# Four products of a residual LoRA kernel, from one float32 pass to three fp32r passes of split parts

## The reference

```
x = x + ((x @ B0[id0].T) @ A0[id0].T)                       # layer 0, rank 16
x = x + (x @ W.T + b) + 2 * ((x @ A1[id1]) @ B1[id1])       # layer 1, W is 2048 x 2048
```

## Time and profile before

| | |
|---|---|
| median of 3 runs | 1398.6 us (1396.78 to 1398.95) |
| profiled execution, its own time | 1398.88 us |
| its span, first to last instruction | 1396.9 us |
| PE busy | 1372.8 us, 98% |
| DVE busy | 943.6 us, 68% |
| ACT busy | 529.1 us, 38% |
| float32 products L540 | 8 records for 4 products |

### The profile page before, as it was taken

One profiled execution on the slowest core, in us unless ns is written; L12 is line 12 of the kernel. 1 busy time (PEld: TensorE's weight loads), 2 busy tenths in 40 slices (PEclk: granted clock), 3 DMA queues, 4 the chain that ended last, 5 costly groups with the idle time before them and its releaser, 6 DMA issues.

```text
span 1396.9 us, 16200 instructions
## 1 busy us (share of the span) xinstructions
PE 1372.8 (98%) x6024; PEld 1128.8 (81%) x6024; DVE 943.6 (68%) x1049; ACT 529.1 (38%) x588; POOL 79.1 (6%) x163
## 2 busy tenths in 40 slices
PE   6899999999999999999999999999999999999999
PEld 5788877888888878888888888888888888888887
DVE  4677897777877887687765566665755566665662
ACT  3444444433334443343324453333233444333321
POOL 2012010001010000001001000000101000000000
PEclk9999999999999999999999999999999999999999
DMA  9789764778888987599895335455856343555642
GB/s 343 242 293 306 264 238 147 243 236 282 297 292 307 314 297 264 178 301 327 287 358 194 110 112 180 163 175 168 276 204 189 117 135 134 169 167 189 194 151 83
DMA packets 98591, 311.60 MB, mean 223 GB/s; under 512 B 13009, under 2 KB 14289, under 8 KB 98513
## 3 DMA queue, kind: packets, MB, share of 16 engines
q1 hardware_dynamic: 92736, 298.96, 63.1%
q0 software_dynamic: 5776, 11.61, 2.9%
HBM read 254.94 MB, written 55.57 MB: 222 GB/s over the span
## 4 chain that ended last, share of the span: by engine, by line
PE 91%; DVE 4%; DMA 2%; issue 1%; ACT 1%; SPq 1%; ACTq 0%; DVEq 0%
PE acc L590 27%; PE acc L591 27%; PE acc L592 27%; DMA w_two<-w 2%; PE acc L565 2%; PE down_ps L549 2%; PE down_ps L550 2%; PE image_ps L535 1%; PE image_ps L529 1%; PE image_ps L530 1%; DVE w_one L759 1%; DVE bg_lo L794 1%; DVE w_lo L767 1%; DVE x_lo L789 0%; ACT w_hi L627 0%
## 5 line engine op out<-in xcount | busy, mean ns | idle before, releaser
L590 PE MATMUL acc<-x_hi,w_hi 128*128 128x512 f32 x1792 | 702.1, 392 | 16.3 <-DVE x_lo L789 12.5
L591 PE MATMUL acc<-x_lo,w_hi 128*128 128x512 f32 x1792 | 699.5, 390 | 0.0
L592 PE MATMUL acc<-x_hi,w_lo 128*128 128x512 f32 x1792 | 699.1, 390 | 0.0
L627 ACT ACTIVATE w_hi<-w_one 128x1024 fp32r<-128x1024 f32 x223 | 235.9, 1058 | 541.1 <-PE acc L592 504.5
L767 DVE TENSOR_TENSOR w_lo<-w_one,w_hi 128x1024 fp32r<-128x1024 f32 x223 | 273.1, 1225 | 215.2 <-ACT w_hi L627 215.2
L590 PEld LDWEIGHTS acc<-x_hi,w_hi 128*128 128x128 f32 x1792 | 337.6, 188 | 89.0 <-issue 16.6
L591 PEld LDWEIGHTS acc<-x_lo,w_hi 128*128 128x128 f32 x1792 | 337.6, 188 | 71.7 <-issue 1.0
L592 PEld LDWEIGHTS acc<-x_hi,w_lo 128*128 128x128 f32 x1792 | 337.3, 188 | 71.2
L660 ACT ACTIVATE sums<-acc 128x512 f32<-128x512 f32 x96 | 57.1, 594 | 203.7 <-PE acc L592 188.1
L826 DVE SCALAR_TENSOR_TENSOR sums<-acc,bias_sb,sums 128x512 f32<-128x512 f32 x128 | 95.7, 747 | 22.0 <-PE acc L565 20.8
L759 DVE TENSOR_TENSOR w_one<-w_one,w_two 128x1024 f32<-128x1024 f32 x79 | 96.4, 1220 | 17.1 <-DMA w_two<-w 17.1
(11 more groups left out here) (61 smaller groups left out, 610.3 us busy)
## 6 DMA issues: line engine op xcount, KB each, us to landing
w_one<-w SPq DMA_DIRECT2D x143, 512.0 KB, 5.5
w_one<-w_sums SPq DMA_DIRECT2D x80, 512.0 KB, 3.7
w_two<-w SPq DMA_DIRECT2D x79, 512.0 KB, 7.4
x_stage<-x SPq DMA_DIRECT2D x64, 512.0 KB, 4.4
out<-sums SPq DMA_DIRECT2D x128, 256.0 KB, 4.6
w_sums<-w_one SPq DMA_DIRECT2D x40, 512.0 KB, 4.1
resident<-x SPq DMA_DIRECT2D x32, 512.0 KB, 8.6
bg_raw<-w_rows SPq DMA_DIRECT2D x32, 512.0 KB, 5.0
```

The lines of the kernel that those rows point to most:

```text
L590: pe.matmul(ps[:, :], w_hi[ws][:, c, :], hi, start=(c == 0), stop=False)
L591: pe.matmul(ps[:, :], w_hi[ws][:, c, :], lo, start=False, stop=False)
L592: mm = pe.matmul(ps[:, :], w_lo[ws][:, c, :], hi, start=False, stop=(c == H - 1))
L627: act.activation(w_hi[s % W_PARTS][:, :, :], w_one[s % W_ONES][:, :, :], ACT.Copy).then_inc(w_hi_ready, 1)
```

## The change

The product of the coupling block with the rows becomes three fp32r matmuls, high x high, low x high and high x low. `across` is split once, both parts on DVE, in its loop body at s = 5, in two more instructions that each wait for the one before. The rows are split for each j at the end of the background splits of the bodies s = 5, 8, 11, 14: ACT makes `rows_hi`, DVE `rows_lo`. The PE no longer waits for the rows' DMAs but for `rows_ready`, which DVE gives behind `rows_lo`; ACT waits for the DMAs, and for j > 0 for the PE's product of j - 1. POOL's load of the next rows waits for `rows_ready` in place of the product.

The raw rows, `across` and the third raw background buffer move into parts of `sums` that aren't yet in use at that time; the memory so freed holds the split parts, with padding so that what follows keeps its place. Because of the third raw buffer, DVE's addition of step 14 now waits until chunk 29 is split.

```diff
+ROWS_SPLIT_AT = (5, 8, 11, 14)
...
-            b1_rows = sb("b1_rows", [P, T], F32, early)
+            across_hi, across_lo = (sb(f"across_{k}", [P, P], F32R, early) for k in ("hi", "lo"))
+            sb("before_image", [P, 2 * P], F32, early)
             image = sb("image", [P, T], F32, early)
-            bg_raw.append(sb("bg_raw2", [P, 2, T], F32, early))
+            rows_hi, rows_lo = (sb(f"rows_{k}", [P, T], F32R, early) for k in ("hi", "lo"))
...
-        across = sums[1][:, H - 1, T - P:T]
+        across = sums[1][:, 1, 0:P]
+        b1_rows = sums[1][:, H - 1, :]
+        bg_raw.append(sums[0][:, H - 2:H, :])
...
             def load_rows(j):
                 if j:
-                    pool.wait_ge(b1_rows_used, j)
+                    pool.wait_ge(rows_ready, j)
...
                     if k == (4 if j else 6):
                         pe.wait_ge(across_ready, 1)
-                        pe.wait_ge(b1_rows_loaded, NB * DMA * (j + 1))
-                        pe.matmul(ps[:, :], across, b1_rows[:, :], start=False, stop=False).then_inc(b1_rows_used, 1)
+                        pe.wait_ge(rows_ready, j + 1)
+                        hi, lo = across_hi[:, :], across_lo[:, :]
+                        pe.matmul(ps[:, :], hi, rows_hi[:, :], start=False, stop=False)
+                        pe.matmul(ps[:, :], lo, rows_hi[:, :], start=False, stop=False)
+                        pe.matmul(ps[:, :], hi, rows_lo[:, :], start=False, stop=False).then_inc(b1_rows_used, 1)
...
                 if s:
                     for z in background(s + 1):
                         split_bg(z)
+                if s in ROWS_SPLIT_AT:
+                    j = ROWS_SPLIT_AT.index(s)
+                    act.wait_ge(b1_rows_loaded, NB * DMA * (j + 1))
+                    if j:
+                        act.wait_ge(b1_rows_used, j)
+                    act.activation(rows_hi[:, :], b1_rows, ACT.Copy).then_inc(rows_hi_ready, 1)
...
                     dve.wait_ge(copied, copied_before(s - H) + 1)
                     if g:
                         dve.wait_ge(out_stored[o], DMA * 4 * g)
+                    elif o == H - 2:
+                        dve.wait_ge(bg_ready, IMAGE - 2)
...
                 if s == 5:
                     dve.wait_ge(across_done, 1)
                     dve.wait_ge(mask_loaded, DMA)
-                    dve.tensor_tensor(across, down_ps[:, 0:P], mask_sb, ALU.mult).then_inc(across_ready, 1)
+                    dve.tensor_tensor(across, down_ps[:, 0:P], mask_sb, ALU.mult).then_inc(across_made, 1)
+                    dve.wait_ge(across_made, 1)
+                    dve.tensor_copy(across_hi[:, :], across).then_inc(across_hi_ready, 1)
+                    dve.wait_ge(across_hi_ready, 1)
+                    dve.tensor_tensor(across_lo[:, :], across, f32(across_hi[:, :]), ALU.subtract).then_inc(across_ready, 1)
+                if s in ROWS_SPLIT_AT:
+                    j = ROWS_SPLIT_AT.index(s)
+                    dve.wait_ge(rows_hi_ready, j + 1)
+                    dve.tensor_tensor(rows_lo[:, :], b1_rows, f32(rows_hi[:, :]), ALU.subtract).then_inc(rows_ready, 1)
```

More of the change, by code:

```diff
@@ L264, in build @@
         across_done = sem("across_done")
+        across_made = sem("across_made")
         across_ready = sem("across_ready")
@@ L267, in build @@
         a0_ready = sem("a0_ready")
+        across_hi_ready = sem("across_hi_ready")
+        rows_hi_ready = sem("rows_hi_ready")
+        rows_ready = sem("rows_ready")
         b1_rows_used = sem("b1_rows_used")
```

## The result

The changed kernel takes 1402.68 us (median of 13 runs, 1399.53 to 1405.25) against 1398.73 us for the kernel before in the same comparison (13 runs, 1396.73 to 1400.62). The ratio is 1.003, 95% interval 1.0023 to 1.0037: slower, by some 4 us. Its profiled execution took 1402.79 us with a span of 1400.8.

The account below looks back on a forecast made before the run. The prediction took the PE to bound the kernel (busy 98%, 91% of the chain). Passes -0.7, wait +3.4 and clock +1.7 sum to +4.4 us, 1403.0 us from a median of 1398.6; range 1399.8 to 1405.0.

Parts of the forecast that it names:

- The wait of j = 1: PE product behind chunk 12 waits for rows_lo, queued behind the split of chunk 14: +3.4 us, some 3.1 idle.
- The passes: Four PE products: three fp32r matmuls take 0.69 us instead of 0.86 for one float32 matmul; -0.7 us in all.
- The upper end that the prediction named for this term: At each product, a gain up to 0.86 - 0.45 = 0.4 us if matmuls ran at half their usual distance.
- Hidden splits: Added ACT and DVE splits at j = 0, 2, 3 cause no PE wait; j = 2 covered by only 0.15 us.
- Rival 4: More PE waits, at j = 2 and in body 5: 1.9 us on the sum, 1404.9 us; chance 0.10.
- Sum of the stretch: Between PE restarts at 68.69 (chunk 5) and 183.55 (first down projection), without clock: -0.7 + 3.4 = +2.7 us.
- The clock: Behind the PE's wait at j = 1 the clock falls to half for 3.4 us: +1.7 us, ends 0 and 3.4.
- a second pause: An extra PE pause at 42 to 44 us, absent behind j = 1; so 3.4 us low expected, against 6.8 seen.
- Rival 1: The wait at j = 1 comes but the clock stays: +2.7 us, 1401.3 us; chance 0.28.
- the advice about gaps: The skill's rule against PE-idle gaps over ~3 us between matmul bursts; the gap at j = 1 at its edge.
- rival 2: Later PE waits for DVE, from 183 us on, shrink and absorb the delay: +0.6 us, 1399.2 us; chance 0.05.
- the least difference a measurement can tell: For the whole kernel's time, about 0.2%, 2.8 us, so slower means over 1401.4 us.

Follow-up runs that it names:

- wait_alone: Kernel before plus only a PE wait: the product of j = 1 also waits for DVE's copy of image 0; 1403.93 us, ratio 1.0037.
- product_later: Changed kernel with the PE's product of j = 1 moved from behind chunk 12 to behind chunk 13; 1398.58 us, ratio 1.0007.
- rows_first: Changed kernel with the rows of j = 1, 2, 3 split ahead of the background splits on ACT and DVE; 1399.43 us, ratio 1.0009.
- one_rows_first: Changed kernel with only the rows of j = 1 split ahead of the background splits; 1397.82 us, ratio 1.0001.
- float32_again: Changed kernel with one float32 matmul of raw parts per product, POOL's load waiting for the product, splits kept; 1403.29 us, ratio 1.0044.
- rows_lo_twice: Changed kernel with DVE doing rows_lo of j = 2 twice; one run, total not given, new PE wait of 0.47 us idle at j = 2.
- splits_no_wait: Changed kernel with float32 products of raw parts, POOL's load waiting for them, and the product of j = 1 behind chunk 13; 1399.26 us, ratio 1.0009.
- long_wait: Kernel before, with the product of j = 1 also waiting for DVE's split of the weights of step 10; 1405.73 us, ratio 1.0047.
- buffers_alone: Kernel before with only the moved raw buffers and DVE's wait in the addition of step 14; 1399.16 us, ratio 1.0001.

## Why the prediction was right, point by point

- **The wait of j = 1.** Forecast: first matmul at 101.15 instead of 97.87, some 3.1 us idle. The trace: 101.26, where 97.95 was due (97.72 + 0.23), 3.16 us idle; the next matmul 0.31 us later instead of 0.23. That is 3.3 + 0.1 = 3.4 us, as forecast. wait_alone shows that it suffices, product_later and rows_first that without it the stretch is 2.7 to 2.8 us shorter.
- **The passes.** Forecast -0.7 us. one_rows_first has -0.85 in the stretch, float32_again against the changed kernel 0.7. Start by start against the kernel before, one_rows_first gains 0.21, 0.22, 0.17 and 0.24 us at the four products. Somewhat better than forecast: the matmuls behind a float32 product also start a little further apart, 2.53 us for eleven starts (98.96 to 101.49 in the kernel before) against 2.50 (98.05 to 100.55 in one_rows_first). The upper end that the prediction named for this term has a slip, since half of 0.69 is 0.35 and not 0.45; nothing else in it uses that number.
- **Hidden splits.** j = 0, 2 and 3 show no wait, j = 2 with 0.1 us to spare beyond the signal (rows_lo_twice) where 0.15 was forecast. Right, and as thin as it said. Rival 4 didn't happen. What the prediction didn't see: behind `rows_lo` of j = 1 the next split comes late, too. In the changed kernel the PE, itself 3.2 us late, doesn't notice; product_later and splits_no_wait pay 0.4 to 0.6 us there.
- **Sum of the stretch.** -0.7 + 3.4 = +2.7 forecast, +2.5 measured.
- **The clock.** The term of the sum that was mis-sized. Forecast +1.7 us, for a fall in the typical execution. The size of one fall was right: 3.4 us at half clock in wait_alone and float32_again. The reason given for that size, a second pause that keeps the clock down longer, isn't borne out: the clock was low for 6.8 us in long_wait, with a single pause, and for 3.4 us in buffers_alone at 40 us, where there are two. So the 3.4 is in part luck. How often it comes was too high: in the changed kernel's own profile the clock stays at 1.00 through this stretch, and over the runs its mean clock is 0.9972 against 0.9980, which by the slope is 0.8 us. Rival 1 and the forecast are thus more likely two kinds of executions of one kernel than two cases, though only the first has a trace: single runs from 1399.5, at 0.999, to 1405.3, at 0.996. Of the advice about gaps that the prediction quotes from the Trainium skill (TensorE: Matmul & The Clock Gate, "Why this matters for your kernels"), the traces here say that a gap of about 3 us is neither safe nor surely bad: of the two gaps at 40 us, 2.84 us in the kernel before and 2.82 in float32_again, the clock fell behind the first and not behind the second.
- **Absorbed later (rival 2).** It didn't come: behind a PE 2.8 us later the wait of the earlier trace rows is 1.03 us in the changed kernel, 0.96 before. What was missed is the other direction, which one_rows_first shows: gain is given back there.
- **What made the total right.** +0.8 of clock instead of +1.7, and +3.6 +- 0.6 at full clock instead of +2.7. The two misses, 0.9 us each way, cancel: that the median came within 0.3 us of the forecast is luck, though either alone would have stayed in the range. In the profiled execution the surplus is 1.0 us of a late weight transfer, and 0.3 at the start. What the surplus in the runs is stays open: all kernels, wait_alone without any split too, lie 0.2 to 1.6 us higher at full clock than their stretches (less the clock's part) say, so it isn't the splits' own; the waits at 200 us, which were 0.96 us in the one trace of the kernel before and 1.2 in the mean of the others, could be part of it.
- **The range and the limit.** No case of the prediction reaches down to 1399.8: rival 1 with the shortest wait gives 1401.0. And the 2.8 us that it took for the least difference a measurement can tell was too cautious: the interval of the ratio is 1.0 us to either side.

**The change without its wait.** one_rows_first is 4 us faster than the changed kernel in the mean, but not measurably faster than the kernel before. Of the 0.85 us that its trace gains in the stretch nothing is left behind the wait of the earlier trace rows, which is 1.0 us longer there; whether it goes the same way in the other runs isn't shown.

## What to carry to other kernels

Before work is put into an engine's queue, ask what stands in front of it there and who must release that. Here the rows stood behind a split that waits for a buffer which the PE frees one instruction before it needs the rows: a circle that doesn't hang, but costs the whole chain of two engines, 3.3 us for the 0.2 us that a cheaper matmul gives; one place earlier on the helpers or one chunk later on the PE removes it, though the second let another 0.6 us through. And a step of a microsecond is settled by the distance between two landmarks in the traces, since totals here scatter by several microseconds with the clock.

## What the runs showed of the hardware

- Whether TensorE's clock falls behind a pause differs between executions: the mean clock of the changed kernel's runs spans 0.996 to 1.0. Behind 3.16 us it stayed at full in the changed kernel's trace and in rows_lo_twice's, and fell to half for 3.4 us in wait_alone's and float32_again's; behind 4.88 us it was low for 6.8 us, in one trace.
- Behind the wait of 2.1 to 3.3 us at 40 us, which all traces but rows_lo_twice's have, it was low for 6.8 us in the kernel before and most others, for 3.4 us in buffers_alone, for some 10 us in product_later, and not at all in float32_again. In rows_lo_twice the wait at 40 us is 0.70 us and the clock stays; there it fell for 3.4 us behind an earlier wait, of 1.88 us at 20.64 (PEclk 0.95 in 20 to 22, 0.50 in 22 to 24, 0.69 in 24 to 26).
- What a fall costs depends on whether the PE waits meanwhile. From the restart at 40 us to chunk 5 it takes 26.77 us in float32_again, with no fall, and also in buffers_alone, where the 3.4 us were over before the PE's next wait ended, at 44.01; it takes 28.39 in the kernel before and 29.52 in product_later. So this place alone spreads the times by 2.8 us.
- A weight transfer of 512 KB issued 1.35 us earlier landed only 0.2 us earlier (11.63 against 10.52 us).
